# Attention with PSUM banks split by purpose: score pairs, single banks for maxima by head, one bank for weighted sums, and GpSimd splitting the maxima

## What is computed

```python
x = x + tanh(g_xattn[0]) * L0_xattn(layernorm(x), ctx, ctx, mask, wq, bq, wk, bk, wv, bv, wo, bo)
x = x + tanh(g_ffn[0])   * L0_ffn(layernorm(x), ...)        # 8 experts, top 2
x = x + tanh(g_xattn[1]) * L1_xattn(layernorm(x), ctx, q_map, k_map, v_map, output_map)
x = x + tanh(g_ffn[1])   * L1_ffn(layernorm(x), weight, bias)   # fp8 fake-quantised

def L1_xattn(q, k, ...):                                    # L0 is the same with biases and a mask
    scores = einsum('brqd,brkd->brqk', qh, kh) * scale
    weights = softmax(scores, axis=-1)
    out = einsum('brqk,brkd->brqd', weights, vh)
```

## Time and profile before

| | |
|---|---|
| runs | 1767.75, 1761.21 and 1768.04 us, median 1767.75 |
| the profiled execution | 1759.03 us, of which the span of instructions is 1757.2 us |
| mean granted TensorE clock over the span | 0.927 of full speed |
| busy over the span | PE 87%, PEld 58%, DVE 73%, ACT 55%, POOL 38% |
| largest groups | DVE's reduces 608.8 us, ACT's exps 522.5 us, PE's values 321.1 us |

### The profile page before, as it was taken

How to read it: one execution, slowest core, us unless ns; L and a number is a source line. 1 busy time by engine, 2 the same in 40 slices (tenths; PEclk the granted TensorE clock), 3 DMA queues, 4 the chain that set the end, 5 groups by cost and what they waited for, 6 DMA issues and landing times. The chain is left out here.

```text
span 1757.2 us, 30430 instructions
## 1 busy us (share of the span) xinstructions
PE 1536.5 (87%) x11934; PEld 1023.1 (58%) x11934; DVE 1275.6 (73%) x1973; ACT 970.1 (55%) x1315; POOL 662.2 (38%) x956
## 2 busy tenths in 40 slices
PE   5776999999979259899999999958869999999865
PEld 4662333333348258899999999934523333333443
DVE  5667999999935756655555554358759999999687
ACT  3443888888844034344445354425527888888545
POOL 3442555555312035433333333244214444454020
PEclk8996999999989569999999999979969999999986
DMA  7653555545362212122123211047644545555102
GB/s 236 234 210 97 124 122 122 119 120 125 87 246 73 72 56 89 40 91 94 47 93 100 82 55 43 31 167 244 232 117 97 124 122 120 120 119 115 41 1 96
DMA packets 117278, 198.71 MB, mean 113 GB/s; under 512 B 28480, under 2 KB 62080, under 8 KB 116112
## 3 DMA queue, kind: packets, MB, share of 16 engines
q1 hardware_dynamic: 83632, 112.30, 20.2%
q0 software_dynamic: 33504, 84.47, 18.7%
HBM read 117.77 MB, written 77.87 MB: 111 GB/s over the span
## 5 line engine op out<-in xcount | busy, mean ns | idle before, releaser
L983 DVE TENSOR_REDUCE a_nmax<-a_ring 128x2 f32<-128x1024 f32 x512 | 608.8, 1219 | 32.2 <-PE a_ring L899 31.9
L970 ACT ACTIVATE i_room<-a_ring 128x1024 f32<-128x1024 f32 x512 | 522.5, 1026 | 145.9 <-PE a_ring L909 145.9
L921 PE MATMUL a_pout<-i_room,values 128*17 128x256 f32 x4096 | 321.1, 386 | 0.7 <-ACT i_room L970 0.7
L1596 ACT ACTIVATE e_full<-e_pH,b1T 128x256 f32<-128x256 f32 x320 | 133.5, 468 | 270.9 <-PE e_pH L1556 270.8
L1625 DVE TENSOR_TENSOR e_hid_lo<-e_full,e_hid_hi 128x512 fp32r<-128x512 f32 x160 | 128.2, 805 | 151.2 <-ACT e_hid_hi L1604 151.2
L1575 PE MATMUL e_pY<-fc_w_hi,e_hid_hi 128*128 128x256 f32 x640 | 185.1, 289 | 8.9 <-DVE e_hid_lo L1625 8.9
L1665 POOL DMA_INDIRECT ytok<-w,slot_put x80 | 78.9, 986 | 298.8 <-DVE w L1640 286.6
L1556 PE MATMUL e_pH<-e_rowsT_hi,fc_w1T_hi 128*128 128x256 f32 x640 | 182.1, 285 | 1.5 <-DVE e_rowsT_lo L1471 1.5
L1556 PE MATMUL e_pH<-e_rowsT_lo,fc_w1T_hi 128*128 128x256 f32 x640 | 181.9, 284 | 0.0
L1556 PE MATMUL e_pH<-e_rowsT_hi,fc_w1T_lo 128*128 128x256 f32 x640 | 181.8, 284 | 0.0
L1575 PE MATMUL e_pY<-fc_w_hi,e_hid_lo 128*128 128x256 f32 x640 | 181.1, 283 | 0.0
(11 more groups left out here) (305 smaller groups left out, 2627.0 us busy)
## 6 DMA issues: line engine op xcount, KB each, us to landing
ks<-i_room SPq DMA_DIRECT2D x64, 256.0 KB
qs<-i_room SPq DMA_DIRECT2D x64, 256.0 KB
outs<-a_osb SPq DMA_DIRECT2D x64, 256.0 KB, 2.7
fc_raw<-in_L_ffn_fc_w SPq DMA_DIRECT2D x16, 1024.0 KB, 6.9
BIG<-outs SPq DMA_DIRECT2D x64, 128.0 KB
ytok<-r_zeros SPq DMA_DIRECT2D x8, 1024.0 KB, 10.2
c_yg<-ytok POOLq DMA_DIRECT2D x16, 512.0 KB, 6.7
i_k<-ks POOLq DMA_DIRECT2D x56, 128.0 KB, 3.3
```

The lines of the kernel that those rows point to most:

```text
L921: mm = e.matmul(pout[n % 2][32 * h:32 * h + VW, at], v[:, b * TPB + t, g * HG + h, :], pexp[t][:, h, at], start=(t == 0 and half == 0), st ...
L970: e.activation(pexp[t][:, 2 * p:2 * p + 2, :], score_bank(n * U + i)[:, :, :], ACT.Exp).then_inc(exped, 1)
L983: e.tensor_reduce(nmax[n % 2][:, :].rearrange("p (x y t) -> p x y t", x=2, y=2)[:, :, p, t], max_bank(m)[:, :, :], AX.X, ALU.max, negate=T ...
L1596: ins = e.activation(full[q % 2][:, f % 2, :], pH[q][:, f % 2, :], ACT.Silu, bias=S.b1T[:, ds(n * KF + f, 1)])
```

## The change

The eight banks are dealt out by purpose. `scores` is two pairs, for score units s alone, in turn. `tops` is three single banks, taken in turn by half units (one head's maxima each, 2m and 2m + 1), so that a reduce now covers one head (128 x 512) and there are twice as many. `pout` is one bank, for which the chunks of a group are packed closer (`LAG`: after score unit 8n + lag comes chunk c of group n). Cutting the maxima moves from DVE to GpSimd (`cut_maxima`), ahead of the loads of each round; DVE turns a group's maxima one unit later than before. AHEAD becomes 16.

```diff
-    AHEAD = 2 * U - 2
-    PAIRED = NG * U - AHEAD
+    AHEAD = 2 * U
+    LAG = ((4, 0), (5, 1), (5, 2), (6, 3), (7, 4), (8, 5), (9, 6), (10, 7))
...
-        ring = [ps(f"ring{j}", [P, 2, SEQ]) for j in range(3)]
-        pout = [ps(f"pout{j}", [P, SEQ]) for j in range(2)]
+        scores = [ps(f"scores{j}", [P, 2, SEQ]) for j in range(2)]
+        tops = [ps(f"tops{j}", [P, SEQ]) for j in range(3)]
+        pout = ps("pout", [P, SEQ])
...
+                def cut_maxima(n):
+                    halves = nparts[n % 2][:, :].rearrange("p (x s c) -> p x s c", x=2, s=2)
+                    whole = nmax[n % 2][:, :].rearrange("p (x c) -> p x c", x=2)
+                    e.wait_ge(reduced, 2 * (n + 1) * U)
+                    if n >= 2:
+                        e.wait_ge(nturned, n - 1)
+                    e.tensor_copy(halves[:, :, 0, :], whole).then_inc(cut, 1)
+                    e.wait_ge(cut, 2 * n + 1)
+                    e.tensor_tensor(halves[:, :, 1, :], whole, halves[:, :, 0, :], ALU.subtract).then_inc(cut, 1)
+
+                cut_maxima(0)
+                cut_maxima(1)
                 inputs.wait_stored(e)
                 for n in range(NG):
+                    if n + 2 < NG:
+                        cut_maxima(n + 2)
                     if n + G < NG:
                         load(n + G)
...
+                    if m:
+                        e.wait_ge(reduced, 2 * m - 1)
                     for hh in range(2):
                         at = slice(HALF * hh, HALF * (hh + 1))
-                        mm = e.matmul(max_bank(m)[:, hh, :], q[j][at, p, t * P:(t + 1) * P], k[j][at, p, :],
-                                      start=True, stop=True)
-                    mm.then_inc(maxed, 1)
+                        e.matmul(tops[(2 * m + hh) % 3][:, :], q[j][at, p, t * P:(t + 1) * P], k[j][at, p, :],
+                                 start=True, stop=True).then_inc(maxed, 1)
...
+                    if s >= 2:
+                        e.wait_ge(exped, s - 1)
...
                 for m in range(AHEAD):
-                    if m >= 3:
-                        e.wait_ge(reduced, m - 2)
                     max_unit(m)
...
+                for s in range(NG * U + U):
+                    if s < NG * U:
+                        score_unit(s)
+                    if AHEAD + s < NG * U:
+                        max_unit(AHEAD + s)
+                    for lag, c in LAG:
+                        if (s - lag) % U == 0 and 0 <= (s - lag) // U < NG:
+                            values((s - lag) // U, c)
...
-                        if i == 3 and n:
+                        if i == 2 and n:
                             take_outputs(n - 1)
...
-                    e.wait_ge(maxed, m + 1)
-                    e.tensor_reduce(nmax[n % 2][:, :].rearrange("p (x y t) -> p x y t", x=2, y=2)[:, :, p, t],
-                                    max_bank(m)[:, :, :], AX.X, ALU.max, negate=True).then_inc(reduced, 1)
+                    columns = nmax[n % 2][:, :].rearrange("p (x y t) -> p x y t", x=2, y=2)
+                    for hh in range(2):
+                        e.wait_ge(maxed, 2 * m + hh + 1)
+                        e.tensor_reduce(columns[:, hh, p, t:t + 1], tops[(2 * m + hh) % 3][:, :], AX.X, ALU.max, negate=True).then_inc(reduced, 1)
...
+                e.memset(pout[:, :], 0.0).then_inc(clear, 1)
                 for m in range(NG * U):
                     reduce(m)
-                    if m < 2:
-                        e.memset(pout[m][:, :], 0.0).then_inc(clear, 1)
-                    if m % U == U - 1:
-                        turn_maxima(m // U)
+                    if m and m % U == 0:
+                        turn_maxima(m // U - 1)
+                turn_maxima(NG - 1)
```

More of the change, by code:

```diff
@@ L809, in attention @@
         oput = [sem(f"oput{j}") for j in range(2)]
[L811 to L815, removed]
         def loaded(e, n):
@@ L896, in max_unit, with score_unit @@
                         loaded(e, n)
+                    if m:
+                        e.wait_ge(reduced, 2 * m - 1)
                     for hh in range(2):
                         at = slice(HALF * hh, HALF * (hh + 1))
-                        mm = e.matmul(max_bank(m)[:, hh, :], q[j][at, p, t * P:(t + 1) * P], k[j][at, p, :],
-                                      start=True, stop=True)
-                    mm.then_inc(maxed, 1)
-                def score_unit(n, i):
+                        e.matmul(tops[(2 * m + hh) % 3][:, :], q[j][at, p, t * P:(t + 1) * P], k[j][at, p, :],
+                                 start=True, stop=True).then_inc(maxed, 1)
+                def score_unit(s):
+                    n, i = s // U, s % U
                     j, t, p = n % G, i // 2, i % 2
@@ L906, in score_unit, with values @@
                         e.wait_ge(mrow[j], 16 * (P // BLOCK) * (n // G + 1))
+                    if s >= 2:
+                        e.wait_ge(exped, s - 1)
                     for hh in range(2):
                         at = slice(HALF * hh, HALF * (hh + 1))
-                        mm = e.matmul(score_bank(n * U + i)[:, hh, :], k[j][at, p, t * P:(t + 1) * P], q[j][at, p, :],
+                        mm = e.matmul(scores[s % 2][:, hh, :], k[j][at, p, t * P:(t + 1) * P], q[j][at, p, :],
                                       start=True, stop=True)
                     mm.then_inc(scored, 1)
[L913 to L917, removed]
+                def values(n, c):
+                    b, g, t, half = n // G, n % G, c // 2, c % 2
+                    if c == 0 and n:
+                        e.wait_ge(taken, n)
                     e.wait_ge(exped, n * U + 2 * t + 2)
@@ L920, in values @@
                     for h in range(HG):
-                        mm = e.matmul(pout[n % 2][32 * h:32 * h + VW, at], v[:, b * TPB + t, g * HG + h, :], pexp[t][:, h, at],
+                        mm = e.matmul(pout[32 * h:32 * h + VW, at], v[:, b * TPB + t, g * HG + h, :], pexp[t][:, h, at],
                                       start=(t == 0 and half == 0), stop=(t == TPB - 1 and half == 1))
@@ L925, in _ @@
                 for m in range(AHEAD):
-                    if m >= 3:
-                        e.wait_ge(reduced, m - 2)
                     max_unit(m)
[L929 to L953, removed]
+                e.wait_ge(clear, 1)
+                for s in range(NG * U + U):
[6 more added lines that the diff above has]
+                            values((s - lag) // U, c)
             @block.scalar
@@ L960, in take_outputs @@
                         e.wait_ge(oput[n % 2], 16 * (n // 2))
-                    e.activation(osb[n % 2][:, :], pout[n % 2][:, :], ACT.Copy).then_inc(taken, 1)
+                    e.activation(osb[n % 2][:, :], pout[:, :], ACT.Copy).then_inc(taken, 1)
                 inputs.wait_stored(e)
@@ L969, in _ @@
                             e.wait_ge(summed, (n - 1) * U + 2 * t + 2)
-                        e.activation(pexp[t][:, 2 * p:2 * p + 2, :], score_bank(n * U + i)[:, :, :], ACT.Exp).then_inc(exped, 1)
-                        if i == 3 and n:
+                        e.activation(pexp[t][:, 2 * p:2 * p + 2, :], scores[i % 2][:, :, :], ACT.Exp).then_inc(exped, 1)
+                        if i == 2 and n:
                             take_outputs(n - 1)
```

## The result

The changed kernel takes 1802.4 us (median of four runs, 1799.7 to 1810.4) against 1764.9 for the kernel before beside it: a ratio of 1.0225, 95% interval 1.0196 to 1.0254. It is slower, as forecast, and inside the forecast's range, but by 37.5 us where the sum of the forecast was 22. The profiled execution has a span of 1800.4 us against 1757.2, so 43.2 us are to be found; part of the distance to 37.5 is that the profiled execution of the kernel before (1759.0 us) was faster than all four of its runs. From the first maximum to the copy of the last output, attention takes 376.8 and 377.4 us in the two layers where it took 354.9 and 356.5: 42.8 of the 43.2 us.

A forecast was written before the change was run, and what follows sets the result against it. Bound before: the loop score, exp, maximum, values, score. Steady groups +5.8, start +5.9, end -0.7 make 11.0 us per layer, 22 for both: 1790 us on the median of 1767.75; range 1755 to 1838, the forecast's own 1762 to 1816.

The forecast's parts named there:

- the loop: Kernel before, steady attention: score, exp, maximum, values, score, closed by the ring of three pairs; 10.40 of a group's 10.53 us.
- Item 1: Steady attention: each maximum waits for the first half reduce of the one before, 0.54 + 0.69 + 0.06 = 1.29 us per unit.
- Item 2: PE, steady groups: the unit with two chunks of values takes 1.65 us against 1.29; the unit without gives nothing back.
- Item 3: Cut moved to GpSimd: 0.6 to 1.0 us, hidden within 1.2; the turn left on DVE adds 0.05 per group.
- Item 5: Steady attention group: 10.73 us against 10.53, +0.20 over some 29 groups, +5.8 us per layer.
- Item 4: GpSimd's loads queue behind the cut: landing after 9.6 to 12.0 us, needed at 12.0; costed at nothing, at most 0.2 per group.
- signs of being wrong: Trace signs: 1.22 us units without DVE waits, reduces at 1.38, turn waiting on GpSimd, or a group's first maximum awaiting a load.
- Item 6: Start of attention: 16 units ahead at half clock, 1.61 us each, +5.9 us per layer; clock assumed to rise after the first score.
- Item 7: End of each layer: sixteen units instead of fourteen run without maxima, at 0.99 us instead of 1.32; -0.7 us per layer.
- Halves that do not overlap: Rival: DVE's two half reduces take 1.38 us per unit and set the pace, group 11.5; 1836 us on the median; chance 0.11.
- Shorter halves: Rival: half reduces of 0.62 us or less, so PE sets the pace at 1.22; 1759 us on the median; chance 0.17.
- GpSimd late: Rival: the cut takes 2.3 us on GpSimd, DVE stands 1.1 per group, loads come later; 1854 on the median; chance 0.08.

The follow-up runs named there:

- e4: The kernel before, with each unit's chunk of values ahead of its maximum pair on PE instead of behind it: 1817.7 us, ratio 1.0294.
- f2: f1 with one chunk of values in every unit: 1752.8 us, ratio 0.9929 to the kernel before.
- e2: The changed kernel with chunks 0 and 1 one unit earlier, so every unit has one chunk of values: 1795.5 us, ratio 1.0176.
- e6: The changed kernel with the cut of the maxima back on DVE, ahead of the turn; GpSimd only loads: 1819.5 us, ratio 1.0306.
- e1: The changed kernel with three of a group's ten loads started before GpSimd's cut and seven after: 1791.9 us, ratio 1.0152.
- e7: The changed kernel with SP's store of a group's outputs held until six scores of the next group are made: 1796.4 us, ratio 1.0192.
- f1: The changed kernel with banks swapped (maxima two pairs, scores three single banks, exps by head), three loads before the cut: 1776.9 us, ratio 1.0059.

## Why the prediction was right, and where it was off

**What bounds the kernel before**: the loop, as far as the runs go. e4 shows that the order on PE can set the pace, f2 that PE was not full at 10.53 us per group; that DVE was not full either is argued. **Item 1, the new loop**: 1.29 us forecast, 1.28 measured; half reduces of 0.68 to 0.69. **Item 2, the long unit**: 0.36 per group forecast (1.65 against 1.29). The two units that follow its chunks take 1.52 and 1.41 instead of 1.28, 0.37 together, and e2's shortest group is 0.35 below the plain one. **Item 3**: right, 0.20 + 0.22 us for the cut, hidden from DVE. **Item 5, the group**: 10.73 forecast, 10.75 measured where no load is late; e6 adds that the cut on GpSimd was needed for that. That the two agree so closely is partly luck: the 0.05 for the turn does not show in the unit behind it (1.29), and 0.14 come from two other units of 1.35 that the sum did not have.

**Item 4 failed in size.** "Just in time; I cost it at nothing, 0.2 us per group as the upper bound" is the term: it measured 0.26 us per group, 15 us. The start of the loads was right, 2.4 us after the last maximum against 2.6 in the sum. The landing was taken from the kernel before; the 2.2 to 4.6 of the earlier trace rows are the ends over all ten loads, and a group's last one took 2.9 to 4.7 there, 3.9 in the median. In the changed kernel it takes 3.8 to 6.4, 4.9 in the median, so the loads arrive 12.1 us after the last maximum in the median, where they are wanted. Then about half are late (26 of 56 opening maxima start within 0.1 us of the landing), and the ends should have been priced as a spread, not as a bound. A maximum waiting for a load is also one of the prediction's own signs of being wrong, and it came. e1 and e6 show that the position behind the cut makes the loads late; of the longer landing e7 explains 0.3 us, and the rest is open.

**Item 6, the start**: 5.9 forecast, 5.3 measured (the loop at the half clock is 1.57, not 1.61). "I let it follow the score" failed: the clock was back 8.2 and 8.8 us after the first score before and 12.1 and 13.2 us after it now, and the first group costs 2.6 and 2.2 us more. **Item 7**: -0.7 forecast, +0.5 per layer measured: around the unit without values and the one with two chunks the last two groups take 0.63, 1.40 and 1.42 us where the kernel before took 0.99 for each unit.

Put together, the terms that the sum had were close: 11.6 forecast for the loop and 11.4 measured, 11.8 and 10.6 for the starts. What it fell short of, 22 against 43.2 us of span, lies in terms that it put at nothing or at less: 15.0 for late loads, 4.8 for the first groups, 2.5 for the ends.

**Rivals.** Halves that do not overlap: refuted, two halves of 0.69 and 0.68 take 1.29 in a row above, 0.61 apart. By the rule of the Trainium skill, "VectorE: DVE Perf Modes", section "The DRAIN you can't avoid", they would stand 0.69 apart; this trace disagrees with that sentence taken alone, as the prediction took it. The section goes on that a next operation that is not held starts earlier, and refers for it to the page's section "Two Vector instructions with no wait between them", by whose model an operation is not held when its inputs and its output start in the same quarter of the partitions as the last ones in that memory. These reduces all read and write from partition 0, and the trace, 0.61 apart, agrees with that. So that page of the Trainium skill as a whole spoke for the forecast's loop, and the rival rested on half of its rule. Shorter halves: refuted, 0.68. GpSimd late: its mechanism did not come on DVE, since its operations cost 0.2, but the loads behind it were late for another reason.

## What to carry to other kernels

When two engines look full, look for the loop: write down from one wait to the next what must happen before PE may write a bank again, and compare that with each engine's own work; e4 shows that exchanging the places of two steps can cost 53 us with nothing added. Splitting a bank's reader in halves shortens its latency but takes away a buffer, so put the single banks where the reader's round is shorter than PE's own (worked out as 1.20 against 1.22 us in f1; 1.29 in the changed kernel), and fill the unit in which that reader does something else (f2). A transfer that is to arrive just in time must be priced with its spread: here it cost 0.26 us per group where nothing was reckoned.

## What the runs showed of the hardware

Back-to-back reduces of 512 columns from PSUM last 0.68 to 0.69 us and start 0.61 apart. The same last load of a group landed 3.9 us after its issue in the kernel before and 4.9 in the changed kernel, where other transfers of the same core start earlier beside it; the 256 KB store, moved by 2 us together with the read-back behind it, changed 0.3 of that. At the start of attention the clock stayed at 0.50 for the whole row 160 to 165 and rose in the row 170 to 175 (0.63) in the changed kernel, where PE had been busy 3.39 of 5 us while it waited for DVE; in the kernel before PE was busy 4.45 us in the row 160 to 165, and the clock rose in the row 165 to 170 (0.70). That the wait for DVE is the cause is argued from these rows, and it is not the whole of it: e2 reaches its first score as late as the changed kernel, 23.8 us after the first maximum, and had the clock back 9.8 and 11.3 us after it instead of 12.1 and 13.2.
